# One-pass shared expert in a two-layer cross-attention kernel on Trainium2

## What is computed

```python
scores = sigmoid(xf @ gate_w + bias)                 # 896 rows, 8 experts
top_scores, top_idx = top_k(scores, 2)
...
up = einsum('th,ehi->tei', xf, up_w) + up_b          # 256 -> 1024
eo = einsum('tei,eih->teh', gelu(up), down_w) + down_b
shared = gelu(xf @ sw_up + sb_up) @ sw_down + sb_down
out = 0.1 * (shared + combined); out = out / max|out|
```

## Time and profile before

| what | us |
|---|---|
| median of three executions | 773.64 |
| the profiled execution | 770.26 |
| its span, first to last instruction | 768.5 |
| TensorE busy in it | 736.5 (96%) |
| ScalarE busy | 379.1 (49%) |
| VectorE busy | 456.4 (59%) |

### The profile page before, as it was taken

The page is one execution under the profiler, slowest core; times in us unless marked ns, Lnnn a source line. Parts: engine busy times, 40 slices in busy tenths (PEclk is TensorE's granted clock), DMA queues, the critical chain, the costliest instruction groups (busy, mean ns, idle before and its releaser), DMA issues.

```text
span 768.5 us, 14883 instructions
## 1 busy us (share of the span) xinstructions
PE 736.5 (96%) x5336; PEld 580.8 (76%) x5336; DVE 456.4 (59%) x1145; ACT 379.1 (49%) x999; POOL 183.8 (24%) x301
## 2 busy tenths in 40 slices
PE   7999999999998999999999999989999988899998
PEld 6567777777776656999999986756767667889976
DVE  3688787877674420223223226757888887897741
ACT  3576766766756321332232324577888787112110
POOL 3032312212000071000000007644554447201000
PEclk9999999999999999999999999999999999999999
DMA  4332323433210973366555522420000000000001
GB/s 163 99 81 66 89 84 105 115 96 99 61 43 18 345 264 107 124 232 226 191 184 174 192 68 85 137 114 2 3 1 3 3 2 2 1 1 1 1 13 36
DMA packets 43532, 69.75 MB, mean 91 GB/s; under 512 B 6611, under 2 KB 35036, under 8 KB 43204
## 3 DMA queue, kind: packets, MB, share of 16 engines
q1 hardware_dynamic: 41924, 65.14, 26.9%
q0 software_dynamic: 1536, 3.67, 1.6%
HBM read 52.56 MB, written 8.26 MB: 79 GB/s over the span
## 4 chain that ended last, share of the span: by engine, by line
PE 75%; DVE 10%; ACT 5%; issue 4%; DMA 3%; POOL 2%; SPq 1%; ACTq 0%; DVEq 0%
PE ps L1399 10%; PE ps L1653 10%; PE ps L1667 9%; PE ps L1869 7%; PE ps L1458 4%; PE ps L1461 4%; PE ps L1577 4%; PE ps L1906 4%; PE ps L1500 3%; PE ps L1751 3%; PE ps L1566 3%; PE ps L1520 2%; PE ps L1471 2%; DVE negmax L951 2%; DMA arena<-arena 2%
## 5 line engine op out<-in xcount | busy, mean ns | idle before, releaser
L752 ACT ACTIVATE OT<-ps,bt 128x128 f32<-128x128 f32 x168 | 48.0, 368 | 104.4 <-PE ps L1653 103.5
L1399 PE MATMUL ps<-ident,arena 112*122 112x112 f32 (+5 forms) x584 | 81.8, 274 | 8.4 <-ACT rt L794 3.5
L1399 PEld LDWEIGHTS ps<-ident,arena 112*122 112x122 f32 (+5 forms) x584 | 63.4, 154 | 32.6 <-issue 17.8
L951 DVE TENSOR_REDUCE negmax<-ps 112x1 f32<-112x375 f32 x128 | 61.2, 541 | 30.0 <-PE ps L1751 29.8
L1653 PE MATMUL ps<-OT,arena 128*128 128x128 f32 x672 | 78.6, 275 | 0.0
L1869 PE MATMUL ps<-arena_r 128*112 128x384 f32 x384 | 75.8, 345 | 1.9 <-DVE acc L1202 1.0
L1653 PEld LDWEIGHTS ps<-OT,arena 128*128 128x128 f32 x672 | 76.8, 192 | 0.4 <-issue 0.3
L1667 PE MATMUL ps<-arena,OT 128*128 128x256 f32 x336 | 75.8, 379 | 0.0
L1127 DVE COPY yo<-ps 128x256 f32<-128x256 f32 x21 | 8.9, 425 | 103.8 <-PE ps L1667 103.8
L1667 PEld LDWEIGHTS ps<-arena,OT 128*128 128x128 f32 x336 | 62.3, 190 | 7.6
L1869 PEld LDWEIGHTS ps<-arena_r 128*112 128x112 f32 x384 | 63.8, 175 | 4.0 <-DVE arena L1341 1.2
(11 more groups left out here) (279 smaller groups left out, 1436.8 us busy)
## 6 DMA issues: line engine op xcount, KB each, us to landing
arena<-in_up_w SPq DMA_DIRECT2D x21, 1024.0 KB, 5.1
arena<-in_down_w SPq DMA_DIRECT2D x8, 1024.0 KB, 12.0
arena<-arena SPq DMA_DIRECT2D x128, 60.9 KB, 2.0
arena<-in_wqkv SPq DMA_DIRECT2D x1, 3072.0 KB, 10.4
arena<-in_ctx SPq DMA_DIRECT2D x8, 375.0 KB
slot_rows<-acc SPq DMA_DIRECT2D x6, 448.0 KB, 3.5
OT<-slot_rows SPq DMA_DIRECT2D x21, 128.0 KB, 2.2
slot_out<-yo SPq DMA_DIRECT2D x21, 128.0 KB, 1.7
```

Source lines behind the costliest of these rows:

```text
L752: act.activation(he[:, i % 2, m, :], ps[:, 2 * (i % 2) + m // 4, (m % 4) * SLOT:(m % 4 + 1) * SLOT], ACT.Gelu, bias=bt[:, i % 3, m:m + 1]) ...
L951: dve.tensor_reduce(negmax[0:TQ, h % 4:h % 4 + 1], ps[0:TQ, S_BANKS[h % 4], 0:TK], AX, ALU.max, negate=True)\
L1399: return pe.transpose(dst, src, ident[0:k, 0:k])
```

## The change

The shared expert's products are made in one pass each, of high and low parts, in the way of the keys and values:

- the rows: ScalarE copies each batch's transposed rows twice, to `xnT_hi` (type `float32r`, in the memory of `OT`) and to `xnT`; VectorE subtracts (`x_low`, in place).
- the weights: four copies of 128x1024 on ScalarE (`sw_high`) to `arena_r`, four subtractions on VectorE (`sw_low`, in place), all in the last batch of layer 0's attention and just behind it.
- the activations: ScalarE applies the activation twice to the same PSUM bank, to `hs_hi` and to `hs`; VectorE subtracts (`hs_low`, in place). `hs` moves to the memory of `w1`.
- `sh_up` has six matmuls instead of two, `sh_down` twelve instead of four. Both wait on one new semaphore, `s_shlo`, that counts all the low parts in VectorE's order (`SH_LOW`).
- The parts in `arena_r` lie over the third buffer of up weights, both of down weights. So SP waits for `s_up` before it loads tile 2's up weights, and VectorE copies the first down weights only when the last `sh_down` is done.
- TensorE's `e_rows(0)` and `e_rows(1)` move behind `sh_down(14)`; `sh_gelu(2)` moves ahead of batch 7's router exponential; the loads of `w1` move from batch 6 of the attention to tiles 8 to 11 of the experts.

```diff
@@ SP
-                    if i == 24:
-                        load_w1(0, "w1q")
-                        load_w1(1, "w1k")
-                    if i == 26:
-                        load_w1(2, "w1v")
-                        load_w1(3, "w1o")
...
             def e_up_load(i):
+                if i == 2:
+                    sp.wait_ge(s_up, 2 * FM)
...
+                if 8 <= i < 12:
+                    load_w1(i - 8, ("w1q", "w1k", "w1v", "w1o")[i - 8])
@@ ScalarE
+                src = ps[:, l0_bank("x", n, 0), 0:KC * TQ].rearrange("p (c q) -> p c q", c=KC)
+                act.activation(xnT_hi[:, :, n * TQ:(n + 1) * TQ], src, ACT.Copy)
+                act.activation(xnT[:, :, n * TQ:(n + 1) * TQ], src, ACT.Copy).then_inc(s_xte, 1)
+            def sw_high(k):
+                if k == 0:
+                    act.wait_ge(L0["v"], 4 * B)
+                    act.wait_ge(s_shw, 64)
+                if k < 2:
+                    act.activation(sw_u_hi[:, k], sw_u[:, k], ACT.Copy).then_inc(s_kvhi, 1)
+                else:
+                    m4 = slice(4 * (k - 2), 4 * (k - 2) + 4)
+                    act.activation(sw_d_hi[:, m4], sw_d[:, m4], ACT.Copy).then_inc(s_kvhi, 1)
...
+                if n == B - 1 and u:
+                    sw_high(u - 1)
+                if n == B - 1 and u == 3:
+                    sw_high(3)
...
+                act.activation(hs_hi[:, u % 4, :], ps[:, u % 2, 0:4 * TQ], ACT.Gelu, bias=upb[:, m:m + 1])
                 act.activation(hs[:, u % 4, :], ps[:, u % 2, 0:4 * TQ], ACT.Gelu, bias=upb[:, m:m + 1]).then_inc(s_gelu, 1)
@@ VectorE
+            def x_low(n):
+                dve.wait_ge(s_rlog, n + 1)
+                q = slice(n * TQ, (n + 1) * TQ)
+                dve.tensor_tensor(xnT_lo[:, :, q], xnT[:, :, q], xnT_hi[:, :, q].bitcast(F32), ALU.subtract)\
+                   .then_inc(s_shlo, 1)
+            def hs_low(u):
+                dve.wait_ge(s_gelu, u + 1)
+                dve.tensor_tensor(hs_lo[:, u % 4, :], hs[:, u % 4, :], hs_hi[:, u % 4, :].bitcast(F32), ALU.subtract)\
+                   .then_inc(s_shlo, 1)
...
-            sh_take(0)
+            for u in range(7, 2 * FM - 1):
+                hs_low(u)
+                if u == 9:
+                    sh_take(0)
+            hs_low(2 * FM - 1)
+            e_rows(0)
+            e_rows(1)
             dve.wait_ge(s_own, 1)
             dve.wait_ge(s_wd, 16 * E0)
+            dve.wait_ge(s_down, 2 * FM)
             e_down_w(0)
+            sh_take(1)
             e_down_w(1)
-            e_rows(0)
-            e_rows(1)
-            sh_take(1)
@@ TensorE
+                pe.wait_ge(s_shlo, SH_LOW.index(("x", 7) if half else ("u", 1)) + 1)
                 if u >= 2:
                     pe.wait_ge(s_gelu, u - 1)
+                q = slice(half * 4 * TQ, (half + 1) * 4 * TQ)
                 for c in range(KC):
-                    ins = pe.matmul(ps[:, u % 2, 0:4 * TQ], sw_u[:, c, m * P:(m + 1) * P],
-                                    xnT[:, c, half * 4 * TQ:(half + 1) * 4 * TQ], start=(c == 0), stop=(c == KC - 1))
+                    for k, (wv, xv) in enumerate(((sw_u_hi, xnT_hi), (sw_u_hi, xnT_lo), (sw_u_lo, xnT_hi))):
+                        ins = pe.matmul(ps[:, u % 2, 0:4 * TQ], wv[:, c, m * P:(m + 1) * P], xv[:, c, q],
+                                        start=(c == 0 and k == 0), stop=(c == KC - 1 and k == 2))
...
-                pe.wait_ge(s_gelu, u + 1)
+                pe.wait_ge(s_shlo, SH_LOW.index(("h", u)) + 1)
...
-                    ins = pe.matmul(dst, hs[:, u % 4, t * TQ:(t + 1) * TQ], sw_d[:, m, :],
-                                    start=(m == 0 and t % 2 == 0), stop=False, skip_group_check=True)
+                    for k, (xv, wv) in enumerate(((hs_hi, sw_d_hi), (hs_hi, sw_d_lo), (hs_lo, sw_d_hi))):
+                        ins = pe.matmul(dst, xv[:, u % 4, t * TQ:(t + 1) * TQ], wv[:, m, :],
+                                        start=(m == 0 and t % 2 == 0 and k == 0), stop=False, skip_group_check=True)
...
+SH_LOW = ([("x", n) for n in range(6)] + [("u", 0), ("u", 1), ("d", 0), ("x", 6), ("h", 0), ("d", 1), ("h", 1), ("h", 2),
+                                          ("x", 7)] + [("h", u) for u in range(3, 16)])
```

More of the change, by code:

```diff
@@ L71, in build @@
         xn = sb("xn", [TQ, B, D])
+        with nc.sbuf_tensor("xnT_r", [P, KC * TOK], F32R) as xnT_r:
+            pass
         xnT = sb("xnT", [P, KC, TOK])
+        with nc.sbuf_tensor("OT_r", [P, 4 * TOK], F32R) as OT_r:
+            pass
         OT = sb("OT", [P, 4, TOK])
@@ L84, in build @@
         rinv = sb("rinv", [P, 4])
+        with nc.sbuf_tensor("wbuf0_r", [P, 2 * FM * D], F32R) as wbuf0_r:
+            pass
         wbuf0 = sb("wbuf0", [P, 2 * FM * D])
@@ L111, in build @@
         yo = sb("yo", [SLOT, 2, D])
+        with nc.sbuf_tensor("w1_r", [P, 4 * KC * D], F32R) as w1_r:
+            pass
         w1 = sb("w1", [P, 4, KC, D])
@@ L224, in build @@
         s_kraw = sem("l0_k_copied")
-        s_kvhi, s_kvlo = sem("l0_kv_high_parts"), sem("l0_kv_low_parts")
+        s_kvhi, s_kvlo, s_shlo = sem("l0_high_parts"), sem("l0_kv_low_parts"), sem("shared_low_parts")
         s_ksw = [sem("l0_k_swapped_even"), sem("l0_k_swapped_odd")]
@@ L731, in _ @@
             l0_x(7)
+            sh_gelu(2)
             l0_r(7)
-            for u in range(2, FM):
+            for u in range(3, FM):
                 sh_gelu(u)
@@ L982, in l0_logits, with sw_low @@
                                   ALU.add).then_inc(s_rz, 1)
+            def x_low(n):
[3 more added lines that the diff above has]
+                   .then_inc(s_shlo, 1)
+            def sw_low(k):
+                dve.wait_ge(s_kvhi, B + k + 1)
+                if k < 2:
+                    ins = dve.tensor_tensor(sw_u_lo[:, k], sw_u[:, k], sw_u_hi[:, k].bitcast(F32), ALU.subtract)
+                else:
+                    m4 = slice(4 * (k - 2), 4 * (k - 2) + 4)
+                    ins = dve.tensor_tensor(sw_d_lo[:, m4], sw_d[:, m4], sw_d_hi[:, m4].bitcast(F32), ALU.subtract)
+                ins.then_inc(s_shlo, 1)
+            def hs_low(u):
+                dve.wait_ge(s_gelu, u + 1)
+                dve.tensor_tensor(hs_lo[:, u % 4, :], hs[:, u % 4, :], hs_hi[:, u % 4, :].bitcast(F32), ALU.subtract)\
+                   .then_inc(s_shlo, 1)
             def kv_low(n):
@@ L1026, in l0_step @@
                     l0_logits(n - 2)
+                    x_low(n - 2)
+                if n == B - 1 and u >= 2:
+                    sw_low(u - 2)
             l0_rope(0, 0)
@@ L1032, in _ @@
             l0_norm(6)
+            sw_low(2)
             l0_logits(6)
+            x_low(6)
+            hs_low(0)
+            sw_low(3)
             l0_rows(7)
+            hs_low(1)
             l0_norm(7)
             l0_logits(7)
+            hs_low(2)
+            x_low(7)
             def bc(v, n):
@@ L1063, in _ @@
             first_largest(rv(3), E0, rv(4), rv(5), io8, rs1[:, 0, :], None, rs1[:, 1, :])
+            hs_low(3)
             link(dve.scalar_tensor_tensor(rt[:, 6, :], rt[:, 4, :], -4.0, rt[:, 3, :], ALU.mult, ALU.add))
@@ L1067, in _ @@
             dve.tensor_tensor(rt[:, 9, :], rt[:, 4, :], rt[:, 7, :], ALU.add).then_inc(s_mask, 1)
+            hs_low(4)
             link(dve.tensor_tensor(rs1[:, 4, :], rs1[:, 0, :], rs1[:, 2, :], ALU.add))
@@ L1075, in _ @@
             dve.tensor_tensor(wtok[:, :, 0:E0], rv(10), bc(rs1[:, 5, :], E0), ALU.mult).then_inc(s_route, 1)
+            hs_low(5)
             dve.wait_ge(s_rank, 1)
@@ L1087, in _ @@
             link(dve.tensor_tensor(sv, rk[:, 0:B * E0].rearrange("p (t e) -> p t e", t=B), bcm(ex[:, 1, :], B), ALU.add))
+            hs_low(6)
             link(dve.tensor_tensor(rt[:, 5, :], rt[:, 4, :], slots[:, :], ALU.mult))
@@ L1628, in _ @@
                 sh_up(u)
-                if u == 2 * FM - 1:
-                    pe.wait_ge(s_idx, 1)
-                    pe.wait_ge(s_wte, 2)
-                    e_rows(0)
-                    e_rows(1)
                 sh_down(u - 1)
@@ L1641, in _ @@
                     w_T(1)
+            pe.wait_ge(s_idx, 1)
+            pe.wait_ge(s_wte, 2)
+            e_rows(0)
+            e_rows(1)
             sh_down(2 * FM - 1)
```

11 lines of the change are left out of this document (7 added, 4 removed).

## The result

The changed kernel took 784.87 us as median of four executions (779.76 to 784.97), the kernel before 774.24 of four (770.73 to 774.86): ratio 1.0118, 95% interval 1.0073 to 1.0163. It is slower by 1.2%, where 766.6 was predicted. The profiled execution took 784.81 us.

What follows compares the result with a forecast made beforehand. TensorE's pace plus its few waits was taken to bound the shared expert. -4.6 - 4.3 + 1.2 + 0.7 = -7.0 us gave 763.3 against the profiled execution, 766.6 against the median; range 762.5 to 771.5 for 8 times in 10.

Steps and rivals of the forecast that it cites:

- sum of -7.0: Whole kernel: -4.6 for `sh_up`, -4.3 for `sh_down`, +1.2 for borders, +0.7 for waits, in us.
- The pace: TensorE in the shared expert: `sh_up` 1.21 us instead of 1.50, `sh_down` 1.46 instead of 1.73, 16 times each.
- The rival of the showing weight loads: Shared expert's matmuls: loads don't overlap streaming, 97 ns more each, +14.8 us, with waits 789; chance 5%.
- the rule of the Trainium skill: TensorE: a weight load overlaps matmuls in flight only when its row group differs; the prediction said the trace disagrees.
- The waits at the tail: End of layer 0's attention and first units: 0.6 us at the start, 0.9 new, 0.8 gone; together +0.7 us.
- The hand-over: From `sh_up` to `sh_down`: a 2.1 us chain of activations and `hs_low`, covered by 2.67 us of TensorE's work; no cost.
- The second rival: Scatter beside `hs_low`: VectorE and POOL hold each other, +1.5 to +4 us, say 769.4; chance 17%.
- The moved loads: Loads of `w1` (1 MB) moved to the experts: join a queue busy for 0.51 of the time, cost nothing.
- The router and the scatter: Stage ahead of `e_rows`: scatter starts 0.6 us earlier and is 1.9 us shorter; rows land with 2.5 us to spare.
- All of it costs nothing: Behind the last `sh_down`: moved down-weight copies, held up-weight loads and `w1` loads add no time.

Runs made afterwards that it cites:

- h3: The changed kernel with POOL waiting ahead of the thirteenth of its 16 scatter steps for the activation of unit 11; 769.76 us, ratio 0.9950.
- k1: The changed kernel with VectorE copying two experts' resident down weights onto themselves behind `hs_low(8)`; 769.74 us, ratio 0.9957.
- f1: The kernel before with only the loads of `w1` moved to tiles 8 to 11 of the experts; 774.73 us, ratio 0.9993.
- f2: The kernel before with VectorE's first down-weight copies moved behind the last `sh_down`, and behind `e_rows`; 783.18 us, ratio 1.0107.
- i2: The program of h3 repeated on another chip, against the kernel before; 775.34 us, ratio 1.0031.
- h1: The changed kernel with POOL waiting ahead of the ninth scatter step for the activation of unit 10; 772.84 us, ratio 0.9958.
- h4: h1 with TensorE's `e_rows(0)` and `e_rows(1)` inside `sh_down(15)`, behind batch 6; 771.63 us, ratio 0.9964.
- k2: h4 with the second `sw_low` behind the normalising of batch 6; 771.86 us, ratio 0.9956.
- a: The changed kernel with the shared expert's products on TensorE in float32 as before, all else kept; 781.27 us, ratio 1.0096.
- g: The changed kernel with float32 products and without the second activations and `hs_low`; 780.65 us, ratio 1.0064.
- before again: The kernel before, unchanged, executed once more; 774.20 us.
- d: The changed kernel with POOL beginning its scatter only behind `sh_down(14)`; 799.12 us in one execution.
- h2: f2 with POOL waiting ahead of the ninth scatter step for the activation of unit 8; 774.90 us, ratio 1.0001.
- i1: The changed kernel repeated on another chip; 780.06 us, ratio 1.0082.
- j1: The changed kernel with a POOL wait ahead of the thirteenth scatter step that was met long before; 781.34 us, ratio 1.0118.

## Why the prediction was wrong

**What was right.** The execution of h3 is the changed kernel as the prediction saw it: no late completion and a clock of 1.00 through the stage. It is the fastest of h3's six executions (the others took 767.37 to 779.55), so it tests the sum and isn't what this kernel usually takes. From the last scores of the attention to the first `e_up`:

```profile
232.66 1.07 PE L1569 MATMUL ps<-arena 64*112 64x487 f32 x4 [1.43 <-DVE arena L972]
...
293.59 0.60 PE L1468 MATMUL ps<-ident,OT 128*128 128x128 f32 x4
...
298.84 3.84 PE L1725 MATMUL ps<-OT,arena 128*128 128x128 f32 x32
```

```profile
241.00:300.20 59.20, 57.68 (x382) 50.32 (x383) 25.17 (x72) 27.75 (x47) 16.91 (x21) 1.00 0.71 236
300.20:458.00 157.80, 157.24 (x1062) 145.50 (x1061) 41.98 (x63) 50.13 (x173) 6.07 (x21) 1.00 0.54 180
```

That is 66.18 us, where the kernel before has 73.52, from this row to 307.21 of the earlier trace rows:

```profile
233.69 1.07 PE L1500 MATMUL ps<-arena 64*112 64x487 f32 x4 [1.43 <-DVE arena L942]
```

-7.3 us against a sum of -7.0, and the execution took 763.21 us against the 763.3 of the sum. That they agree so closely is in part luck, since one term came out 0.5 us better and another 0.6 worse. Term by term:
- The pace. Units of the changed kernel at full clock, in the timeline:

```profile
303.63 0.37 PE L1636 MATMUL ps<-OT_r,arena_r 128*128 128x448 f32 x1
...
304.86 0.28 PE L1648 MATMUL ps<-arena_r 128*112 128x256 f32 x1
...
306.27 0.37 PE L1636 MATMUL ps<-OT_r,arena_r 128*128 128x448 f32 x1
```

  `sh_up` 1.23 and `sh_down` 1.41 us, where 1.21 and 1.46 were predicted: 2.64 instead of 2.67. A matmul of 256 columns costs 118 ns, so 11 above its columns. The rival of the showing weight loads had 0.284 and 0.204 a matmul; it falls, and with it, for this kernel, the rule of the Trainium skill that the prediction cites beside it.
- The waits at the tail: `sh_up(0)` comes 1.4 us late (0.6 predicted), 241.61 - 232.66 against 241.27 - 233.69; the 0.78 us wait for `hs_low(3)` is as predicted (0.6). Together some 0.6 us more than the +0.7 of the sum.
- The hand-over is hidden, as said: no other wait for L1029 at full clock.
- The second rival, VectorE and POOL holding each other, is real but small. A scatter step that starts while `hs_low` runs is longer. In h3 this is one step, 1.25 us instead of 0.94:

```profile
277.34 0.63 DVE L1031 TENSOR_TENSOR w_r<-w,arena_r 128x448 fp32r<-128x448 f32 x1 [5.20 <-ACT w L753]
277.54 1.25 POOL L469 DMA_INDIRECT slot_rows<-xn,sloti  x1 [0.30 <-issue]
```

  In k1 it is three steps, of 1.08 to 1.19 us, together 0.5 us; in the changed kernel's trace no step starts so. `hs_low` itself always takes 0.62 or 0.63 us. The prediction had priced this rival at 1.5 to 4 us; `e_rows` didn't wait for it in h3 or k1.
- The moved loads cost nothing that can be seen (f1: 0.9993, 0.9972 to 1.0015), and the experts keep their length: 298.84 to 454.02, so 155.18 us, where before had 155.19.

**The step that failed** is in "The router and the scatter": "that copy is now behind the last `sh_down`, so the scatter is also 1.9 us shorter", counted as a gain, and "All of it costs nothing" for the moved copies. The 1.9 us were won and worth nothing (`e_rows` had spare time), and the stop that went with them had kept the completions on time. What showed it: f2 (only this moved, +8.3 us), k1 (copies of that size put back, 769.7 instead of 780 to 785), i2 (completions come while the scatter stands).

**What the prediction didn't think of** is the clock. The sum takes every matmul at 2.4 GHz, with no term for anything else. Over its 108 executions the kernel before has a mean clock of 0.992, and 0.001 of it goes with 0.64 us (a line through them). The changed kernel's first four have 0.979: 0.013 x 640 = 8 us. Part of that follows from the wait (in f2 the clock falls behind it, 0.988). Part is there without it: five versions without late completions in their profiled execution (h1, h3, h4, k1, k2; 49 executions) have 0.9877 and a mean of 771.0 us. So in means, at equal clock (the line taken to 0.99):

| | us | at clock 0.99 |
|---|---|---|
| before | 774.3 | 775.4 |
| without late completions | 771.0 | 769.5 |
| changed, first four | 783.6 | 776.4 |

By this estimate the products bring 5.9 us, the late completions take 6.9, the lower clock 8.3: 9.3 in all, as the means say. The rows come from different chips, and three of the five versions in the second one (h1, h3, h4) from the chip on which nothing was late; k1 and k2 alone give 770.1 at clock 0.99, so 5.3 us for the products. Of the 5.9 another 2.6 go to the clock even without the late completions. Why the clock is lower with one-pass products isn't settled. With float32 ones and all else of the change it is 0.990 (a, g), though these two have the waits too; k1, with one-pass ones, has 0.991. The falls stand behind waits (291.9 above) and in dense stretches (278.3) alike, and between executions of one kernel they vary as much as between kernels.

**Left open** is why a scatter in one piece makes completions late, and why not in each execution (none in the profiled ones of h2 and h3). One more observation bears on it. In most executions the trace lacks records of semaphore increments there (increments that the engines make in 272 to 297 us, and those recorded; "wait" is TensorE's longest amid the units):

```
                 made  recorded  longest wait us
before             29        29  0.8
before again       30        17  0.8
changed            27        21  8.2
a                  28        15  4.0
f2                 20        11  5.5
d (no scatter)     38        38  0.8
h1                 40        40  0.8
h2                 28        28  0.8
h3                 41        41  0.8
h4                 37        37  0.8
i1                 23        17  8.3
i2                 27        19  2.7
k1                 39        28  0.8
k2                 36        23  0.8
```

In 200 to 250 and in 330 to 440 us none is missing in any of them. Beside POOL's other row of indirect transfers, which gathers the experts' outputs (460 to 496 us), some are again, 21 of 102 in the changed kernel, and none in the five executions that lack none beside the scatter (before, h1 to h4). So records are lost beside indirect transfers, in the kernel before as well, and late increments are seen only in executions that lose records. All four on the chip of h1 to h4 lose none, with the scatter in one piece (h2, h3) or not. So on that chip the effect may be absent whatever the program, and the argument rests on f2, g, k1 and k2 on one chip and i1, i2 and j1 on another. The Trainium skill, "NOTIFIC — the notification-queue block", section "Overflow: three behaviours, one of which stalls the engine", says that the block which records such events holds its producers back rather than lose a record inside, and that by its setting it discards records or stalls the producer when a queue's ring is full. By that the recording itself could be what makes them late. The lateness agrees with a stall and the missing records with a discard; no run shows the setting, and no execution here was free of recording, so this rival is untested. It wasn't tried whether the scatter's 1 KB rows, their number or the transfers beside them matter.

## What to carry to other kernels

A thing that stops another engine for 2 us may be what keeps a third on time: where a copy or a wait moves out of a stretch with a long row of indirect transfers, run that move by itself first. When a wait is longer than the work that it waits for, lay the producer's timeline beside the waiter's: if the producer had finished long ago, no duration explains it. And take the granted clock of several executions of before as a term of the sum: here 0.001 of it goes with 0.64 us, and the medians of the kernel before on four chips lie up to 3 us apart.

The better versions of those tried are the changed kernel with the scatter stopped by the copy (k1) or tied to the units (k2; h1 and h4 on the chip where nothing was late): 0.4% faster than before, where the products alone are worth some 0.7 to 0.8%.
